# Transposing x on TensorE instead of through a DRAM copy and a DMA transpose, in an eight-core attention and quantised feed-forward kernel

## Chip, cores and metric

One Trainium2 chip, eight cores, one program. The 16 sequences are split two to a core; the cores exchange nothing. The metric is the device time in microseconds of the slowest core.

## The reference

For each sequence of 2048 tokens with 1024 features, in float32 (cut):

```python
q = x @ Wq.T + bq;  k = x @ Wk.T + bk;  v = x @ Wv.T + bv
scores = where(j > i, -inf, q @ k.T / 32)
attn = softmax(scores, axis=-2)
x = layernorm(x + attn @ v)
h = bit_linear(x, w1)                 # activations to 8 bits, weights to -1, 0, 1
h = silu(depthwise_conv1d(h) + conv_b)
x = layernorm(x + bit_linear(h, w2))
```

Every projection contracts over the 1024 features, so TensorE needs x with the features on the partitions, that is x transposed.

## The kernel before

The program is a list of operations with named resources; `Prog.build` turns the dependences into semaphore waits, engine by engine, in program order. Three of its rules matter here. A DMA waits for the DMA issued before it on the same engine's queue, so each queue has one transfer in flight. A DMA transpose (`xbar=True`) also waits for the last DMA of every other queue, and every later DMA waits for it. `fence(new, old)` makes the first use of each new name wait for all users of the old names, where two sets of tiles share memory.

Constants and zero padding come first (POOL issues 36 tiny stores, L352 to L362). Then the three attention weights are staged: eight tiles each of 128 rows are loaded by SP (L384), cast to bf16 by DVE (L387) and stored to DRAM by POOL (L390). Then `attn(b)` runs for the core's two sequences:

1. For 16 row tiles of x: SP loads 512 KB into `A_x32[it % 2]` (L397), DVE casts it into `A_xbf[it % 2]` (L400), POOL stores 256 KB to `s_xbf` in DRAM (L403). Then the bias row `bv` is loaded (L409) and spread over the partitions by PE and DVE (L413, L417).
2. SP transposes `s_xbf` into eight tiles `A_xT[e8]` of 128 features by 2048 tokens (L421, eight DMA transposes), then Wv into `A_WvT` (L431, eight more), and for the first sequence Wq and Wk too.
3. V (L442, 256 matmuls), Q and K (L461, 512 matmuls), each reading `A_xT`.
4. Scores and exponentials into `A_P`, which shares memory with `A_xT`, `A_WvT` and the bias tiles (L497 to L540).
5. The attention output, first layernorm and quantisation, by row tile (L560 on). Each tile ends with `pv_xpose_flush`: eight PE transposes (L551), by turns into the PSUM tiles `X6` and `X7`, eight ACT copies out of them (L555), and a POOL store.

After both sequences `prep()` quantises w1 and w2, `ffn_entry()` brings them in by DMA transposes, and 16 chunks of the feed-forward follow (L838 to L969).

Of the kernel before, what the change touches and what calls it, by code (L numbers as in the profile page):

```python
# [19 lines left out]
ECH = 8  # L20
# [144 lines left out]
def build_program(T=2048, NB=2, debug=False):  # L165
    nc = bass.Bass("TRN2", target_bir_lowering=False)
    NT = T // 128
    NCHUNK = T // 256
    p = Prog()
# [24 lines left out]
    s_xbf = dscr("s_xbf", [NB, T, E], BF16)  # L194
# [28 lines left out]
    iden_bf = P_("iden_bf", [128, 128], BF16)  # L223
# [29 lines left out]
    def mc(i):  # L253
# [3 lines left out]
    A_xT = [mem.at(OB + e * 4096, f"A_xT{e}", [128, T], BF16) for e in range(ECH)]  # L257
# [10 lines left out]
           for t in range(NT)]  # L268
# [6 lines left out]
    A_xbf = [mem.at(AT + 8192 + i * 2048, f"A_xbf{i}", [128, E], BF16)  # L275
             for i in range(2)]
# [47 lines left out]
    B = [pstack.enter_context(nc.psum_tensor(f"bank{i}", [128, 512], F32))  # L324
         for i in range(6)]
    X6 = pstack.enter_context(nc.psum_tensor("xb6", [128, 1024], BF16))
    X7 = pstack.enter_context(nc.psum_tensor("xb7", [128, 1024], BF16))
# [4 lines left out]
         writes=["idenf"])  # L332
# [3 lines left out]
         reads=["idenf"], writes=["maskneg"])  # L336
# [3 lines left out]
         reads=["idenf"], writes=["idenf"])  # L340
    p.op("DVE", lambda e: e.tensor_copy(out=iden_bf[:], in_=iden_f[:]),
         reads=["idenf"], writes=["idenb"])
# [7 lines left out]
    for b in range(NB):  # L350
        for e8 in range(ECH):
            p.op("POOL", lambda e, b=b, e8=e8: e.dma_start(  # L352
                out=s_xqT[b, e8, :, 0:8], in_=zpad[:]),
                reads=["zpad"], writes=[f"sxq_zh{b}_{e8}"], dma=True)
            p.op("POOL", lambda e, b=b, e8=e8: e.dma_start(
                out=s_xqT[b, e8, :, T + 8:T + 16], in_=zpad[:]),
                reads=["zpad"], writes=[f"sxq_zt{b}_{e8}"], dma=True)
    for b in range(NB):
        p.op("POOL", lambda e, b=b: e.dma_start(
            out=s_m1[b, 0:1].rearrange("(o a) -> o a", o=1), in_=misc[0:1, 60:61]),  # L360
            reads=["msczero"], writes=[f"sm1z{b}"], dma=True)
# [30 lines left out]
                reads=[f"xbf{i % 2}"], writes=[f"scr_{nm}_{i}"], dma=True)  # L392

    def attn(b):
        for it in range(NT):
            sl = slice(it * 128, (it + 1) * 128)
            p.op("SP", lambda e, sl=sl, it=it: e.dma_start(  # L397
                out=A_x32[it % 2][:], in_=x_d[b, sl, :]),
                writes=[f"x32_{it % 2}"], dma=True)
            p.op("DVE", lambda e, it=it: e.tensor_copy(  # L400
                out=A_xbf[it % 2][:], in_=A_x32[it % 2][:]),
                reads=[f"x32_{it % 2}"], writes=[f"xbf{it % 2}"])
            p.op("POOL", lambda e, sl=sl, it=it: e.dma_start(  # L403
                out=s_xbf[b, sl, :], in_=A_xbf[it % 2][:]),
                reads=[f"xbf{it % 2}"], writes=[f"sxbf{it}"], dma=True)
        p.fence([f"xT{e}" for e in range(ECH)]
                + [f"WvT{e}" for e in range(ECH)] + ["BVbc", "bvrow"],
                [f"P{jt}" for jt in range(NT)])
        p.op("SP", lambda e: e.dma_start(out=A_brow2[:],  # L409
                                         in_=bv_d.rearrange("(o a) -> o a", o=1)),  # L410
             writes=["bvrow"], dma=True)
        for h in range(2):
# [4 lines left out]
            p.op("DVE", lambda e, h=h: e.tensor_copy(  # L417
                out=A_BVbc[:, h * 512:(h + 1) * 512], in_=B[h][:]),
                reads=[f"B{h}"], writes=["BVbc"])
        for e8 in range(ECH):  # L420
            p.op("SP", lambda e, e8=e8: e.dma_start(  # L421
                out=A_xT[e8][:], in_=s_xbf[b, :, e8 * 128:(e8 + 1) * 128],
                transpose=True),
                reads=[f"sxbf{it}" for it in range(NT)],
                writes=[f"xT{e8}"], dma=True, xbar=True)
        wlist = [(s_wv, A_WvT, "WvT", "wv")]
        if b == 0:
            wlist += [(s_wq, A_WqT, "WqT", "wq"), (s_wk, A_WkT, "WkT", "wk")]
# [8 lines left out]
        for it in range(NT):  # L437
            g = it % 2
            bk0, bk1 = 2 * g, 2 * g + 1
            for h, bk in ((0, bk0), (1, bk1)):  # L440
                for e8 in range(ECH):
                    p.op("PE", lambda e, it=it, h=h, bk=bk, e8=e8: e.matmul(  # L442
                        out=B[bk][:],
                        lhsT=A_xT[e8][:, it * 128:(it + 1) * 128],
                        rhs=A_WvT[e8][:, h * 512:(h + 1) * 512],
                        start=(e8 == 0), stop=(e8 == ECH - 1)),
                        reads=[f"xT{e8}", f"WvT{e8}"], writes=[f"B{bk}"])
                p.op("DVE", lambda e, it=it, h=h, bk=bk: e.tensor_tensor(
                    out=A_v[it][:, h * 512:(h + 1) * 512], in0=B[bk][:],
                    in1=A_BVbc[:, h * 512:(h + 1) * 512], op=ALU.add),  # L450
                    reads=[f"B{bk}", "BVbc"], writes=[f"v{it}"])

        icw = min(512, T)
        for dstl, wTl, bc, nm in ((A_qT, A_WqT, bqc, "q"), (A_kT, A_WkT, bkc, "k")):
            wkey = "WqT" if nm == "q" else "WkT"
            for fc in range(ECH):
                for ic in range(T // icw):
                    bk = (fc * (T // icw) + ic) % 4
                    for e8 in range(ECH):
                        p.op("PE", lambda e, fc=fc, ic=ic, bk=bk, e8=e8,  # L460
                             wTl=wTl: e.matmul(  # L461
                            out=B[bk][:, 0:icw],
                            lhsT=wTl[e8][:, fc * 128:(fc + 1) * 128],
                            rhs=A_xT[e8][:, ic * icw:(ic + 1) * icw],
                            start=(e8 == 0), stop=(e8 == ECH - 1)),
                            reads=[f"xT{e8}", f"{wkey}{e8}"], writes=[f"B{bk}"])
                    p.op("ACT", lambda e, fc=fc, ic=ic, bk=bk, dstl=dstl,
                         bc=bc: e.activation(
                        out=dstl[fc][:, ic * icw:(ic + 1) * icw],
                        in_=B[bk][:, 0:icw],  # L470
                        func=AF.Identity, bias=bc[:, fc:fc + 1], scale=1.0),
                        reads=[f"B{bk}", "b" + nm + "c"],
                        writes=[f"{nm}T{fc}"])

        p.fence([f"P{jt}" for jt in range(NT)],
                [f"xT{e}" for e in range(ECH)] + [f"WvT{e}" for e in range(ECH)]
                + ["BVbc", "BVbc_use", "brow", "bvrow"])
        gchunk = 0
        for jt in range(NT):
# [175 lines left out]
    def prep():  # L655
# [2 lines left out]
                [f"P{jt}" for jt in range(NT)] + [f"v{t}" for t in range(NT)]  # L658
                + [f"qT{e}" for e in range(ECH)] + [f"kT{e}" for e in range(ECH)]
                + [f"WqT{e}" for e in range(ECH)] + [f"WkT{e}" for e in range(ECH)]  # L660
                + [f"WvT{e}" for e in range(ECH)] + [f"xT{e}" for e in range(ECH)]
                + ["xres", "xln0", "xln1", "xqstg", "xqbf", "pvx0", "pvx1",
                   "BVbc", "bvrow", "brow", "x32_0", "x32_1", "xbf0", "xbf1"])
        tiles = []
# [90 lines left out]
    def ffn_entry():  # L755
        newk = ([f"W1qT{e}" for e in range(ECH)]
                + [f"W2qT{c}" for c in range(HCH)]
                + [f"Fg{pr}_{s}" for pr in range(2) for s in range(HCH)]
                + [f"F_xq{pr}_{e}" for pr in range(2) for e in range(ECH)]
                + [f"fxlnt{pr}_{t}" for pr in range(2) for t in range(2)]  # L760
                + [f"fw{pr}" for pr in range(2)] + [f"fbc{pr}" for pr in range(2)]
                + ["sbc", "fs2seg", "Mx", "Mn", "flnt"]
                + [f"hs{i}" for i in range(2)] + [f"u{i}" for i in range(2)]
                + [f"fev{i}" for i in range(2)]
                + [f"D{k}_{pr}" for k in range(3) for pr in range(2)]
                + ["fcm0", "fcm1", "fcn0", "fcn1", "fm2", "fr2", "fs2v", "frs2"])
        oldk = ([f"P{jt}" for jt in range(NT)] + [f"v{t}" for t in range(NT)]
                + [f"qT{e}" for e in range(ECH)] + [f"kT{e}" for e in range(ECH)]
                + [f"xT{e}" for e in range(ECH)] + [f"WqT{e}" for e in range(ECH)]
                + [f"WkT{e}" for e in range(ECH)] + [f"WvT{e}" for e in range(ECH)]  # L770
                + ["xres", "xln0", "xln1", "xqstg", "xqbf", "pvx0", "pvx1",
                   "BVbc", "bvrow", "brow", "x32_0", "x32_1", "xbf0", "xbf1"]
                + [f"pin{i}" for i in range(4)] + [f"pap{u}" for u in range(32)]
                + ["pob0", "pob1", "m1ct", "mrow"]
                + [f"cmax{i}" for i in range(4)] + [f"csum{i}" for i in range(4)]
                + ["colsum", "msczero", "Mraw"])
        p.fence(newk, oldk)
        for e8 in range(ECH):
            p.op("SP", lambda e, e8=e8: e.dma_start(
                out=F_W1qT[e8][:], in_=s_w1i[:, e8 * 128:(e8 + 1) * 128],  # L780
                transpose=True),
                reads=[f"sw1ib{i}" for i in range(16)],
                writes=[f"W1qT{e8}"], dma=True, xbar=True)
        for c in range(HCH):
            p.op("SP", lambda e, c=c: e.dma_start(
                out=F_W2qT[c][:], in_=s_w2i[:, c * 128:(c + 1) * 128],
                transpose=True),
                reads=[f"sw2ib{i}" for i in range(16)],
                writes=[f"W2qT{c}"], dma=True, xbar=True)
# [358 lines left out]
```

How the kernel before makes its waits and increments, by code:

```python
            def section(_):  # L118
                waited = {f: 0 for f in self.ENGINES}
                for i, emit, inc, deps in ops:
                    want = {}
                    for d in deps:
                        f = openg[d]
                        v = cums[d]
                        if v > want.get(f, 0):
                            want[f] = v
                    for f, v in want.items():
                        if waited[f] < v:
                            eo.wait_ge(sems[f], v)
                            waited[f] = v
                    inst = emit(eo)
                    if inc:
                        inst.then_inc(sems[streams[i]], inc)
```

## Time and profile before

| | us |
|---|---|
| median of 2 runs | 3677.25 (3653.91 and 3700.6) |
| profiled execution, device time | 3621.03 |
| its span, slowest core (core 1) | 3619.5 |
| spans of the eight cores | 3602.0 to 3619.5 |

The span is the time from the first to the last instruction of a core; the other 1.5 us of the profiled execution lie around it. Engines are PE (TensorE), DVE (VectorE), ACT (ScalarE), POOL (GpSimd) and SP; a name with a q after it is the engine's instruction queue, where DMAs are issued. The chain of waits is followed back from the last instruction: at each step to what released it.

### The profile page before, as it was taken

To read this page: it belongs to the slowest core of one execution; us is meant where nothing else is said; L and a number is where in the kernel's file an instruction comes from. 1 tells how busy PE (TensorE), PEld (TensorE's weight loads), DVE (VectorE), ACT (ScalarE), POOL (GpSimd) and SP (SyncE) were. 2 spreads that over 40 slices of the span, in tenths; PEclk is the share of its full clock that TensorE was granted. 3 is DMA by queue.
4 is the path that set the end of the run, shared out by engine and by line. 5 is a ranking of instruction groups with operands and counts; after the bars stand their busy time and mean duration, and the time that the engine had idled before them with its cause. 6 is when DMAs were issued, how large, how long until landed. Compare 5 with 4: busy or idle time off the path is not lost.

```text
span 3619.5 us, 39595 instructions; the slowest of 8 cores (3602.0 to 3619.5 us)
## 1 busy us (share of the span) xinstructions
PE 2036.9 (56%) x10824; PEld 1128.8 (31%) x10824; DVE 1409.0 (39%) x3969; ACT 1208.1 (33%) x3042; POOL 185.1 (5%) x297
## 2 busy tenths in 40 slices
PE   0006984630996471000018777877777877778775
PEld 0002431210443120000005454544444544445442
DVE  0112025530204553333006544555544555554554
ACT  0000423320132332332006444444444444444442
POOL 2100000110000110011000000000000000000000
PEclk9999996765998575555558888877888878788887
DMA  0554002345000235876630000000000000000000
GB/s 25 197 169 76 1 1 73 105 129 130 6 1 12 93 108 197 294 260 201 124 76 23 30 30 24 19 19 30 30 30 25 18 18 30 30 30 27 16 18 18
DMA packets 201374, 248.20 MB, mean 69 GB/s; under 512 B 143106, under 2 KB 159682, under 8 KB 192964
## 3 DMA queue, kind: packets, MB, share of 16 engines
q1 hardware_dynamic: 174468, 138.61, 14.2%
q0 software_dynamic: 22080, 73.50, 5.9%
q10 hardware_dynamic: 4608, 33.56, 2.8%
q8 instruction: 92, 1.51, 0.2%
q14 instruction: 126, 1.03, 0.1%
HBM read 138.58 MB, written 73.48 MB: 59 GB/s over the span
## 4 chain that ended last, share of the span: by engine, by line
PE 36%; DMA 24%; DVE 17%; issue 10%; ACT 10%; POOL 1%; DVEq 1%; ACTq 0%; POOLq 0%; SPq 0%
PE bank L957 11%; PE bank L838 9%; PE bank L461 6%; DVE F_u L945 4%; DMA PR_in<-w 3%; PE bank L859 3%; PE bank L442 3%; DVE Fg L948 3%; DMA F_W2qT<-s_w2i 3%; DMA s_xbf<-A_xbf 3%; DMA s_w2i<-PR_ob 2%; DMA s_w1i<-PR_ob 2%; PE bank L497 2%; ACT F_D L851 2%; DMA A_xT<-s_xbf 2%
## 5 line engine op out<-in xcount | busy, mean ns | idle before, releaser
L838 PE MATMUL bank<-F_xq,F_W1qT 128*128 128x258 bf16 x4096 | 652.0, 312 | 0.0
L957 PE MATMUL bank<-F_W2qT,Fg 128*128 128x512 bf16 x2048 | 526.2, 395 | 45.6 <-ACT F_ev L969 39.2
L838 PEld LDWEIGHTS bank<-F_xq,F_W1qT 128*128 128x128 bf16 x4096 | 453.4, 111 | 180.6 <-issue 27.9
L864 ACT ACTIVATE Fg<-bank,cbc 128x256 bf16<-128x256 f32 x512 | 241.7, 472 | 741.0 <-PE bank L859 732.7
L859 PE MATMUL bank<-F_hs,F_D 128*128 128x256 bf16 x1536 | 286.8, 301 | 226.2 <-DVE F_hs L844 108.3
L844 DVE TENSOR_TENSOR F_hs<-bank,F_fbc 128x258 bf16<-128x258 f32 x512 | 217.1, 424 | 338.1 <-PE bank L859 306.6
L826 PE MATMUL bank<-F_fw,ones 1*128 1x258 f32 x32 | 18.6, 680 | 485.2 <-DVE F_fw L822 485.2
L957 PEld LDWEIGHTS bank<-F_W2qT,Fg 128*128 128x128 bf16 x2048 | 203.4, 100 | 261.6 <-issue 93.2
L859 PEld LDWEIGHTS bank<-F_hs,F_D 128*128 128x128 bf16 x1536 | 144.4, 104 | 312.6 <-issue 287.1
L876 DVE TENSOR_TENSOR F_Mx<-F_Mx,Fg 128x256 bf16<-128x256 bf16 x496 | 143.5, 289 | 204.7 <-ACT Fg L864 201.4
L945 DVE TENSOR_TENSOR F_u<-Fg,F_sbc 128x256 f32<-128x256 bf16 x512 | 214.1, 418 | 0.6
L851 ACT ACTIVATE F_D<-iden_f,w0c 128x128 bf16<-128x128 f32 x512 | 200.0, 391 | 17.2 <-DMA s_w2i<-PR_ob 17.2
L851 ACT ACTIVATE F_D<-iden_f,w1c 128x128 bf16<-128x128 f32 x512 | 199.3, 389 | 0.0
L851 ACT ACTIVATE F_D<-iden_f,w2c 128x128 bf16<-128x128 f32 x512 | 199.3, 389 | 0.0
L573 PE MATMUL bank<-A_v,A_P 128*128 128x512 bf16 x544 | 174.0, 489 | 28.4 <-DVE misc L531 14.5
L442 PE MATMUL bank<-A_WvT,A_xT 128*128 128x512 bf16 x512 | 121.2, 397 | 121.4 <-DMA A_WvT<-s_wv 121.4
L948 DVE TENSOR_SCALAR Fg<-F_u 128x256 bf16<-128x256 f32 x512 | 150.5, 294 | 56.8 <-DVE F_u L945 3.2
L413 PE MATMUL bank<-A_brow,ones 1*128 1x512 f32 x8 | 7.5, 1089 | 285.7 <-DMA A_brow<-bv 285.7
L497 PE MATMUL bank<-A_qT,A_kT 128*128 128x512 bf16 (+3 forms) x640 | 138.4, 373 | 45.1 <-ACT A_P L525 41.7
L826 PEld LDWEIGHTS bank<-F_fw,ones 1*128 1x128 f32 x32 | 7.7, 299 | 489.3 <-issue 489.3
L551 PE MATMUL xb<-iden_bf,PV_xqbf 128*128 128x128 bf16 x256 | 60.1, 249 | 172.8 <-DVE PV_xqbf L637 132.6
L879 DVE TENSOR_TENSOR F_Mn<-F_Mn,Fg 128x256 bf16<-128x256 bf16 x496 | 141.5, 285 | 0.7 <-DVE F_Mx L876 0.7
(131 smaller groups left out, 2003.4 us busy)
## 6 DMA issues: line engine op xcount, KB each, us to landing
PR_in<-w ACTq DMA_DIRECT2D x32, 1024.0 KB, 6.8
PR_in<-w SPq DMA_DIRECT2D x32, 1024.0 KB
A_x<-x SPq DMA_DIRECT2D x32, 512.0 KB
PV_xsrc<-x SPq DMA_DIRECT2D x32, 512.0 KB
s_xln<-PV_xln POOLq DMA_DIRECT2D x32, 512.0 KB, 3.3
F_xlnt<-s_xln SPq DMA_DIRECT2D x32, 512.0 KB
out<-F_xlnt POOLq DMA_DIRECT2D x32, 512.0 KB, 3.0
F_xq<-s_xqT SPq DMA_DIRECT2D x128, 64.5 KB
```

What stands on the lines that cost most here:

```text
L442: p.op("PE", lambda e, it=it, h=h, bk=bk, e8=e8: e.matmul(out=B[bk][:], lhsT=A_xT[e8][:, it * 128:(it + 1) * 128], rhs=A_WvT[e8][:, h * 51 ...
L461: wTl=wTl: e.matmul(out=B[bk][:, 0:icw], lhsT=wTl[e8][:, fc * 128:(fc + 1) * 128], rhs=A_xT[e8][:, ic * icw:(ic + 1) * icw], start=(e8 == ...
L497: p.op("PE", lambda e, e8=e8, jt=jt, cs=cs, w=w, bk=bk: e.matmul(out=B[bk][:, 0:w], lhsT=A_kT[e8][:, jt * 128:(jt + 1) * 128], rhs=A_qT[e8 ...
L573: p.op("PE", lambda e, it=it, jt=jt, h=h, bk=bk: e.matmul(out=B[bk][:], lhsT=A_P[jt][:, it * 128 - jt * 128: it * 128 - jt * 128 + 128], r ...
L838: p.op("PE", lambda e, s=s, e8=e8, bk=bk, par=par: e.matmul(out=B[bk][:, 0:258], lhsT=F_W1qT[e8][:, s * 128:(s + 1) * 128], rhs=F_xq[par][ ...
L844: p.op("DVE", lambda e, s=s, bk=bk, par=par: e.tensor_tensor(out=F_hs[s % 2][:], in0=B[bk][:, 0:258], in1=F_fbc[par][:], op=ALU.mult), rea ...
L851: p.op("ACT", lambda e, k=k, s=s, wc=wc: e.activation(out=F_D[k][s % 2][:], in_=iden_f[:], func=AF.Identity, scale=wc[:, s:s + 1]), reads= ...
L859: p.op("PE", lambda e, k=k, s=s: e.matmul(out=B[2][:, 0:256], lhsT=F_D[k][s % 2][:], rhs=F_hs[s % 2][:, k:k + 256], start=(k == 0), stop=( ...
L864: p.op("ACT", lambda e, s=s, par=par: e.activation(out=F_g[par][s][:], in_=B[2][:, 0:256], func=AF.Silu, bias=cbc[:, s:s + 1], scale=1.0), ...
L945: p.op("DVE", lambda e, cs=cs, par=par, up=up: e.tensor_tensor(out=F_u[up][:], in0=F_g[par][cs][:], in1=F_sbc[:], op=ALU.mult), reads=[f"F ...
L948: p.op("DVE", lambda e, cs=cs, par=par, up=up: e.tensor_scalar(out=F_g[par][cs][:], in0=F_u[up][:], scalar1=MAGIC, scalar2=MAGIC, op0=ALU. ...
L957: p.op("PE", lambda e, par=par, tb=tb, h=h, cs=cs, bk=bk: e.matmul(out=B[bk][:], lhsT=F_g[par][cs][:, tb * 128:(tb + 1) * 128], rhs=F_W2qT ...
```

## The change

Step 2 loses the transposes of x, and step 1 loses the stores. In the loop over the 16 row tiles, each cast tile is transposed by PE in eight blocks of 128x128, by turns into `X6` and `X7`, and ACT copies each block into its place in `A_xT[e8]`. The names `xT{e8}` become `xT{e8}_{t}`, one per row tile. Because `A_xT` is now written inside the loop, the fence against `A_P` moves ahead of the loop, and it now also covers `x32_0`, `x32_1`, `xbf0` and `xbf1`. The loads, the casts, the load of `bv`, the transposes of the weights and all matmuls of V, Q and K stay.

```diff
     def attn(b):
+        p.fence([f"xT{e}_{t}" for e in range(ECH) for t in range(NT)]
+                + [f"WvT{e}" for e in range(ECH)] + ["BVbc", "bvrow",
+                   "x32_0", "x32_1", "xbf0", "xbf1"],
+                [f"P{jt}" for jt in range(NT)])
         for it in range(NT):
...
-            p.op("POOL", lambda e, sl=sl, it=it: e.dma_start(
-                out=s_xbf[b, sl, :], in_=A_xbf[it % 2][:]),
-                reads=[f"xbf{it % 2}"], writes=[f"sxbf{it}"], dma=True)
-        p.fence([f"xT{e}" for e in range(ECH)]
-                + [f"WvT{e}" for e in range(ECH)] + ["BVbc", "bvrow"],
-                [f"P{jt}" for jt in range(NT)])
+            for e8 in range(ECH):
+                xb = X6 if e8 % 2 == 0 else X7
+                xk = "X6" if e8 % 2 == 0 else "X7"
+                p.op("PE", lambda e, it=it, e8=e8, xb=xb: e.transpose(
+                    out=xb[:, 0:128],
+                    in_=A_xbf[it % 2][:, e8 * 128:(e8 + 1) * 128],
+                    identity=iden_bf[:]),
+                    reads=[f"xbf{it % 2}", "idenb"], writes=[xk])
+                p.op("ACT", lambda e, it=it, e8=e8, xb=xb: e.copy(
+                    out=A_xT[e8][:, it * 128:(it + 1) * 128], in_=xb[:, 0:128]),
+                    reads=[xk], writes=[f"xT{e8}_{it}"])
...
-        for e8 in range(ECH):
-            p.op("SP", lambda e, e8=e8: e.dma_start(
-                out=A_xT[e8][:], in_=s_xbf[b, :, e8 * 128:(e8 + 1) * 128],
-                transpose=True),
-                reads=[f"sxbf{it}" for it in range(NT)],
-                writes=[f"xT{e8}"], dma=True, xbar=True)
...
-                        reads=[f"xT{e8}", f"WvT{e8}"], writes=[f"B{bk}"])
+                        reads=[f"xT{e8}_{it}", f"WvT{e8}"], writes=[f"B{bk}"])
```

The reads of the Q and K matmuls and the later fences take the new names.

## Rows read from the trace of the kernel before

**Rows 1.** The page: span; busy time; busy tenths in 40 slices; chain by engine and line.
```profile
span 3619.5 us, 39595 instructions; the slowest of 8 cores (3602.0 to 3619.5 us)
PE 2036.9 (56%) x10824; PEld 1128.8 (31%) x10824; DVE 1409.0 (39%) x3969; ACT 1208.1 (33%) x3042; POOL 185.1 (5%) x297
PE   0006984630996471000018777877777877778775
PE 36%; DMA 24%; DVE 17%; issue 10%; ACT 10%; POOL 1%; DVEq 1%; ACTq 0%; POOLq 0%; SPq 0%
PE bank L957 11%; PE bank L838 9%; PE bank L461 6%; DVE F_u L945 4%; DMA PR_in<-w 3%; PE bank L859 3%; PE bank L442 3%; DVE Fg L948 3%; DMA F_W2qT<-s_w2i 3%; DMA s_xbf<-A_xbf 3%; DMA s_w2i<-PR_ob 2%; DMA s_w1i<-PR_ob 2%; PE bank L497 2%; ACT F_D L851 2%; DMA A_xT<-s_xbf 2%
```

**Rows 2.** Chain of waits around the first sequence's x: start us, us, what.
```profile
227.92 0.50 issue
228.42 3.14 DMA s_xbf<-A_xbf
...
238.99 2.31 DMA s_xbf<-A_xbf
241.39 0.04 issue
241.43 4.38 DMA A_xT<-s_xbf
...
272.14 4.51 DMA A_xT<-s_xbf
276.71 3.37 DMA A_WvT<-s_wv
...
300.78 3.46 DMA A_WvT<-s_wv
304.23 0.14 issue
304.37 15.79 PE bank L442 x62
```

**Rows 3.** Timeline, first sequence: start us, us, engine, line, what, count [idle before <-releaser].
```profile
173.34 57.95 SPq L397 DMA_DIRECT2D A_x<-x  x16
234.86 0.24 SPq L409 DMA_DIRECT2D A_brow<-bv  x1
236.60 3.75 PE L413 MATMUL bank<-A_brow,ones 1*128 1x512 f32 x4 [223.09 <-DMA A_brow<-bv]
241.43 32.69 SPq L421 DMA_TRANSPOSE A_xT<-s_xbf  x8
276.71 25.21 SPq L431 DMA_TRANSPOSE A_WvT<-s_wv  x8
```

**Rows 4.** Timeline, second sequence: from the end of the attention before to WvT.
```profile
751.45 7.07 PE L573 MATMUL bank<-A_v,A_P 128*128 128x512 bf16 x32
778.94 1.27 DVE L400 CAST A_xbf<-A_x 128x1024 bf16<-128x1024 f32 x2
779.69 56.69 SPq L397 DMA_DIRECT2D A_x<-x  x14
787.42 0.53 POOL L648 DMA_DIRECT2D s_m<-mrow  x1 [6.73 <-DMA s_xqT<-PV_xqstg]
789.70 0.59 POOL L403 DMA_DIRECT2D s_xbf<-A_xbf  x1 [1.75 <-DMA s_m<-mrow]
792.23 0.69 DVE L400 CAST A_xbf<-A_x 128x1024 bf16<-128x1024 f32 x1 [12.02 <-DMA s_xbf<-A_xbf]
839.65 0.25 SPq L409 DMA_DIRECT2D A_brow<-bv  x1
841.26 3.75 PE L413 MATMUL bank<-A_brow,ones 1*128 1x512 f32 x4 [62.63 <-DMA A_brow<-bv]
847.22 32.69 SPq L421 DMA_TRANSPOSE A_xT<-s_xbf  x8
882.21 26.10 SPq L431 DMA_TRANSPOSE A_WvT<-s_wv  x8
```

**Rows 5.** SP's queue, single load issues: weights, then the second sequence's x.
```profile
13.21 0.36 SPq L384 DMA_DIRECT2D A_x<-wq  x1
17.84 0.35 SPq L384 DMA_DIRECT2D A_x<-wq  x1
21.71 0.33 SPq L384 DMA_DIRECT2D A_x<-wq  x1
25.57 0.33 SPq L384 DMA_DIRECT2D A_x<-wq  x1
...
784.02 0.33 SPq L397 DMA_DIRECT2D A_x<-x  x1
793.00 0.33 SPq L397 DMA_DIRECT2D A_x<-x  x1
```

**Rows 6.** Timeline and one line's instructions: the last transposes and copies after the attention.
```profile
775.34 0.39 PE L551 MATMUL xb<-iden_bf,PV_xqbf 128*128 128x128 bf16 x2 [9.13 <-DVE PV_xqbf L637]
775.69 3.13 ACT L555 COPY PV_xqstg<-xb 128x128 bf16<-128x128 bf16 x8 [4.44 <-PE xb L551]
L555 ACT COPY PV_xqstg<-xb x256: 265/266/268, 591.6 to 1383.4; 128x128 bf16<-128x128 bf16 x128
```

**Rows 7.** Stages by window: us, busy (x) of each engine, PEclk, DMA share, GB/s.
```profile
178.00:241.40 63.40, 3.75 (x4) 1.16 (x4) 12.37 (x18) 0.00 (x0) 9.17 (x17) 1.00 0.58 195
241.40:276.70 35.30, 0.00 (x0) 0.00 (x0) 0.00 (x0) 0.00 (x0) 0.00 (x0) 1.00 0.61 119
1935.00:2040.00 105.00, 81.08 (x489) 51.47 (x489) 56.96 (x189) 49.61 (x142) 1.70 (x3) 0.84 0.05 15
2355.00:2460.00 105.00, 79.95 (x459) 49.45 (x458) 54.82 (x183) 47.42 (x134) 2.26 (x4) 0.80 0.08 26
```

More of the change, by code:

```diff
@@ L465, in attn @@
                             start=(e8 == 0), stop=(e8 == ECH - 1)),
-                            reads=[f"xT{e8}", f"{wkey}{e8}"], writes=[f"B{bk}"])
+                            reads=[f"xT{e8}_{ic * icw // 128 + t}"
+                                   for t in range(icw // 128)]
+                            + [f"{wkey}{e8}"], writes=[f"B{bk}"])
                     p.op("ACT", lambda e, fc=fc, ic=ic, bk=bk, dstl=dstl,
@@ L475, in attn @@
         p.fence([f"P{jt}" for jt in range(NT)],
-                [f"xT{e}" for e in range(ECH)] + [f"WvT{e}" for e in range(ECH)]
+                [f"xT{e}_{t}" for e in range(ECH) for t in range(NT)]
+                + [f"WvT{e}" for e in range(ECH)]
                 + ["BVbc", "BVbc_use", "brow", "bvrow"])
@@ L660, in prep @@
                 + [f"WqT{e}" for e in range(ECH)] + [f"WkT{e}" for e in range(ECH)]
-                + [f"WvT{e}" for e in range(ECH)] + [f"xT{e}" for e in range(ECH)]
+                + [f"WvT{e}" for e in range(ECH)]
+                + [f"xT{e}_{t}" for e in range(ECH) for t in range(NT)]
                 + ["xres", "xln0", "xln1", "xqstg", "xqbf", "pvx0", "pvx1",
@@ L768, in ffn_entry @@
                 + [f"qT{e}" for e in range(ECH)] + [f"kT{e}" for e in range(ECH)]
-                + [f"xT{e}" for e in range(ECH)] + [f"WqT{e}" for e in range(ECH)]
+                + [f"xT{e}_{t}" for e in range(ECH) for t in range(NT)]
+                + [f"WqT{e}" for e in range(ECH)]
                 + [f"WkT{e}" for e in range(ECH)] + [f"WvT{e}" for e in range(ECH)]
```

## The prediction

> **What bounds the kernel now.** I read the page first. TensorE has the largest share of busy time, 56% of the span, but its row of 40 slices shows stretches where it does nothing at all, and the chain of waits puts 24% of the span on DMAs [rows 1]. So no one engine bounds the kernel; it goes from stage to stage, and each has its own limit. Among the chain's lines two belong to the operations that the change removes: the stores `s_xbf<-A_xbf` at 3% and the transposes `A_xT<-s_xbf` at 2% of 3619.5 us.
>
> Second I read the chain in order of time around the first sequence [rows 2]. From about 182 to 241 us it runs from store to store, then through eight transposes of x, then through eight of Wv, and only then into the V matmuls (L442). Nothing else is on it. Third, the windows: from 241.4 to 276.7 us not one of the five engines is busy for any time [rows 7]. The transposes of x hide nothing and nothing hides them.
>
> Fourth, the timelines of both sequences give the times at which the DMAs are issued [rows 3, 4]. These are what the sum is made from, because all that follows the first issue of `A_WvT` (its eight transposes, V, Q, K) is the same before and after.
>
> **First sequence.** The first transpose of Wv is issued at 276.71 us. After the change it waits for the load of `bv` on its own queue, and for the last POOL DMA, which is then a weight store long finished. `bv` is issued at 234.86 and released PE at 236.60 [rows 3]. If the loads of x keep their pace, the first Wv transpose is issued at 236.6: 276.7 - 236.6 = 40.1 us earlier. It has two parts: 276.71 - 241.43 = 35.3 for the eight transposes of x, and 241.43 - 236.60 = 4.8 for the last stores, which ran on behind `bv`.
>
> **Do the loads keep their pace?** The 16 loads and the wait of the last reach from 173.34 to 234.86, 61.5 us or 3.85 each [rows 3]. The chain runs through the stores, so the loads might be held back by them. But SP's queue shows weight loads of the same size at a time when POOL stores only 2 KB pieces: issued at 17.84, 21.71 and 25.57, so 3.87 and 3.86 apart [rows 5]. I take 3.85: load and store happened to be equally slow, and taking the store away leaves the load. What it costs the other way is a rival below.
>
> **What is added per tile.** Eight PE transposes and eight ACT copies, 128 of each per sequence. The same work stands after the attention, with the same alternation of `X6` and `X7`: eight copies from first start to last end in 3.13 us, each 0.266 us long, so one every (3.13 - 0.27)/7 = 0.41 us, and the first transpose starts 0.35 us ahead of the first copy [rows 6]. A tile alone takes 0.35 + 3.13 = 3.5 us; in a steady stream 8 x 0.41 = 3.3 us. Both are below 3.85, PE and ACT have nothing else to do then (PE busy 3.75 us and ACT 0 of 63.4 [rows 7]), and two `A_xbf` buffers let tile it+1 be cast while tile it is transposed. I cost them at nothing. The cover is the load; without it they would cost the 3.3 us a tile. The last tile's 3.5 us and PE's 3.75 us for the bias rows (L413) come after the last load, some 8 us with the cast, but they lie beside the eight Wv transposes, which take 304.2 - 276.7 = 27.5 us [rows 2]. The first V matmul needs the first of these, but its group ends with the eighth. An activation table load at ACT's first instruction falls in the wait for the first tile.
>
> **Second sequence.** Here a further stall goes. DVE's third cast waits 12.02 us for a store of x, which stood on POOL's queue behind the store of `s_m`, which had waited 6.73 us for the store of `s_xqT` [rows 4]. SP therefore issues its load at 793.00 and not some 3.9 us after the one at 784.02 [rows 5]. With no store of x the cast needs only the load and the PE transposes two tiles before. The 14 loads from 779.69 then take 4.33 (to 784.02, as seen) and 13 x 3.85 = 50.1 us: `bv` is issued at 834.1 instead of 839.65. It lands 841.26 - 839.65 = 1.6 us later, at 835.7, and the Wv transpose that was issued at 882.21 is issued then: 46.5 us earlier. Its parts are 882.21 - 847.22 = 35.0 for the transposes of x, 847.22 - 841.26 = 6.0 for the last stores, 5.6 for the stall.
>
> **The moved fence.** The first two loads of the second sequence now wait for the last attention matmul, which ends at 751.45 + 7.07 = 758.5 us. Behind them on SP's queue stand only the other loads of x. Two loads at 4.63 at most (the slowest issue to issue, 13.21 to 17.84 [rows 5]) land by 767.8, and DVE cannot cast before 778.94, when its own queue is through with the layernorm [rows 4]. Cost nothing, with 11 us to spare; were that cover gone, each load would cost its 3.85. For the first sequence the fence is empty. The finer names `xT{e8}_{t}` add at most waits that are already satisfied: PE has waited for nearly all the copies when it transposes the last tile.
>
> **The sum.** 40.1 + 46.5 = 86.6 us. Against the profiled execution: 3621.0 - 86.6 = 3534 us. The median of the runs shown is 56 us above that execution, and the two runs differ by 47 us, so against the median it is 3677.25 - 86.6 = 3590.6 us, 2.4% less. I give 3591. A difference of 2%, about what a measurement of this kernel can tell from no change, is 73.5 us.
>
> **A page against the trace.** The eight transposes of x take 4.4 us each for 512 KB [rows 2], at 119 GB/s [rows 7]. The Trainium skill (DMA: Bandwidth & Descriptors, section Latency and other measured facts) gives DMA transposes an effective 261 GB/s, which would be an estimated 2.0 us each. By the page the sum would be 86.6 - 70.3 + 32 = 48 us, within 2%; the trace has the duration itself, and it decides.
>
> **The rivals.**
>
> *The loads speed up.* The stores did: the last one, with no load beside it, took 2.31 us where the one at 228.42 took 3.14 [rows 2]. If the loads fell below 3.3 us, the copies would set the pace at 3.28, and 14 + 13 tiles would each save 0.57 us: 15.4 us more, 102 in all, 3575 us. Against it speak the weight loads at 3.86 [rows 5]. Chance 0.14. Beside it stands a rule of the Trainium skill (DMA: Bandwidth & Descriptors, section Anatomy of one DMA, measured on the GpSimd path): 2.0 us plus the bytes over 436 GB/s, here an estimated 3.2 us for a load. The 3.86 of the rows disagrees with it.
>
> *The hand-over per tile costs more.* PE and ACT wake each other 16 times a tile. If the pace came to 4.3 us, 0.45 x 29 tiles = 13 us would go, and the change would fall within 2%; at 5 us the gain is 86.6 - 33 = 53 us, 3624. For it speaks how little lies between 3.5 and 3.85; against it, that eight copies in the same pattern kept 0.41 us. Chance 0.11.
>
> *The feed-forward's clock.* It is half of the span, and its granted clock, a mixture of the levels 1.2 and 2.4 GHz, lies between 0.80 and 0.84 in stretches of 105 us, with PE 80 us busy [rows 7]. A mean lower by 0.02 costs up to 80 x 0.02/0.82 = 2.0 us in each of 16, 31 us in all, and leaves 55: 3622 us. Nothing in the change reaches that stage, but the runs shown differ by as much. Chance 0.08.
>
> *The stages of a tile stop overlapping,* the way to a slower kernel. If load, cast, transposes and copies ran one after the other, a tile would cost 3.85 + 0.69 + 3.5 = 8.0 us, 4.2 more, 122 us over 29 tiles: 35 us slower than before, 3713. It decides from 86.6/29 = 3.0 us more a tile, that is 6.85, and is slower by 2% only from 9.4. Against it stand the two buffers for x and for the cast. Chance 0.02.
>
> *The transposes were hidden anyway.* The empty window [rows 7] excludes it but for 0.01.
>
> **How the numbers follow.** The likeliest, 0.64, is the sum, with a gain of 77 to 93 us. Faster by over 2% takes nearly all of it (0.62) and the faster loads (0.14): 0.76. Within 2%: 0.02 of the first, 0.11, 0.08, 0.01 and most of the serial case: 0.23. Slower: 0.01. The range runs from the sum against the profiled execution, 3534, rounded down to 3530 for loads that gain a little, up to 3640, which holds the slow hand-over and the clock. It leaves out the serial case, the hidden one, and the faster loads where they fall together with runs as fast as the profiled one.
>
> **What would show it.** In the changed profile `s_xbf<-A_xbf` and `A_xT<-s_xbf` are gone, 128 transposes and copies per sequence lie between the loads, and these still come 3.85 us apart: right on the pace. The first Wv transpose at about 237 us and, 86.6 us earlier than before, at about 796 in the second sequence: right on the sum. No 12 us wait of a cast: right on the stall. Casts that wait for PE, or PE for ACT, with loads over 4.3 us apart, would show the hand-over wrong. The Q and K matmuls and the feed-forward should last as long as before; if they don't, the sum is wrong in a place it doesn't look at.

## The result and the profile after

The changed kernel takes 0.968 of the time of the kernel before (95% interval 0.965 to 0.972): medians of all runs 3520.7 and 3627.3 us, about 115 us by the ratio. In some executions one die ran at a lower granted clock and took longer; the medians count them, the ratios here do not. The profiled executions took 3512.2 and 3621.0 us; their spans, as means over the eight cores, are 3499.4 and 3608.2, 108.8 us apart. Faster was forecast, but by 87 us and not under 3530: the gain is larger by a quarter to a third, and the time lies below the range.

The page of the changed kernel, its span, busy times and the chain by line; the two entries that [rows 1] shows for `s_xbf` are gone:

```profile
span 3510.7 us, 40780 instructions; the slowest of 8 cores (3488.6 to 3510.7 us)
PE 2097.0 (60%) x11080; PEld 1155.2 (33%) x11080; DVE 1408.5 (40%) x3969; ACT 1267.2 (36%) x3298; POOL 167.0 (5%) x265
PE bank L965 11%; PE bank L846 9%; PE bank L464 6%; DVE F_u L953 4%; PE bank L867 3%; DMA PR_in<-w 3%; PE bank L445 3%; DVE Fg L956 3%; DMA A_x<-x 3%; DMA F_W2qT<-s_w2i 3%; DMA s_w1i<-PR_ob 3%; PE bank L503 3%; DMA s_w2i<-PR_ob 2%; ACT F_D L859 2%; DMA s_xqT<-zpad 2%
```

Its chain of waits around the first sequence's x (start us, us, what), the counterpart of [rows 2]:

```profile
203.59 3.34 DMA A_x<-x
...
214.03 3.13 DMA A_x<-x
...
217.28 3.35 DMA A_x<-x
...
220.70 1.56 DMA A_brow<-bv
222.30 0.04 issue
222.34 3.17 DMA A_WvT<-s_wv
```

The chain now goes from load to load, and from `bv` straight to Wv. SP's queue of the same core, both sequences, beside [rows 3, 4]:

```profile
165.75 51.85 SPq L401 DMA_DIRECT2D A_x<-x  x16
220.70 0.24 SPq L418 DMA_DIRECT2D A_brow<-bv  x1
222.34 25.34 SPq L434 DMA_TRANSPOSE A_WvT<-s_wv  x8
...
705.09 69.55 SPq L401 DMA_DIRECT2D A_x<-x  x16
778.08 0.25 SPq L418 DMA_DIRECT2D A_brow<-bv  x1
779.65 20.95 SPq L434 DMA_TRANSPOSE A_WvT<-s_wv  x7
```

From these marks, as means over the eight cores, comes the table on which the rest of this text leans. The last column is the prediction's term.

| stretch | before | after | gained | forecast |
|---|---|---|---|---|
| start to the first load of x (the weights) | 171.9 | 164.1 | 7.8 | 0 |
| 16 loads of x, to the issue of `bv` | 62.4 | 54.9 | 7.5 | 0 |
| `bv` to the first Wv transpose | 42.2 | 1.5 | 40.7 | 40.1 |
| to `bv` of the second sequence | 563.2 | 555.3 | 7.9 | 5.6 |
| `bv` to Wv, second sequence | 43.2 | 1.6 | 41.6 | 40.9 |
| to the quantisation of w1 | 505.7 | 503.8 | 1.9 | 0 |
| to the feed-forward and its end | 2219.6 | 2218.2 | 1.4 | 0 |

The transposes and the waits for the last stores went as worked out. Of the 22 us that the sum does not have, 15 lie in the DMAs ahead of them, and 8 of these where the two programs do the same.

How close the added work comes to being the limit stands in the waits of the changed kernel, 170 to 222 us (who waited for whom, us in total, times, longest):

```profile
DVE A_xbf L404 <- DMA A_x<-x: 22.0, 8, 3.4
...
PE xb L410 <- ACT A_xT L415: 17.8, 50, 1.7
DVE A_xbf L404 <- PE xb L410: 15.7, 6, 2.9
```

Eight casts waited last for their load, six for the transposes two tiles back; the chain above still goes from load to load without a break. PE transposes in pairs, 0.77 us from pair to pair, 3.1 us a tile, against a load every 3.43. The work is hidden, but only by 0.3 us a tile.

### The profile page after: what moved, and what is told of

It reads as the page before. It is cut to its first block, busy times and chain, and to the rows that moved or that the text cites. A ratio compares the mean times of both kernels' runs of the same rounds, so it can differ in the third digit from the quotient of the medians.

```text
span 3510.7 us, 40780 instructions; the slowest of 8 cores (3488.6 to 3510.7 us)
## 1 busy us (share of the span) xinstructions
PE 2097.0 (60%) x11080; PEld 1155.2 (33%) x11080; DVE 1408.5 (40%) x3969; ACT 1267.2 (36%) x3298; POOL 167.0 (5%) x265
## 4 chain that ended last, share of the span: by engine, by line
PE 38%; DMA 23%; DVE 18%; ACT 10%; issue 9%; POOL 1%; DVEq 1%; ACTq 0%; POOLq 0%; SPq 0%
PE bank L965 11%; PE bank L846 9%; PE bank L464 6%; DVE F_u L953 4%; PE bank L867 3%; DMA PR_in<-w 3%; PE bank L445 3%; DVE Fg L956 3%; DMA A_x<-x 3%; DMA F_W2qT<-s_w2i 3%; DMA s_w1i<-PR_ob 3%; PE bank L503 3%; DMA s_w2i<-PR_ob 2%; ACT F_D L859 2%; DMA s_xqT<-zpad 2%
## 5 line engine op out<-in xcount | busy, mean ns | idle before, releaser
L410 PE MATMUL xb<-iden_bf,A_xbf 128*128 128x128 bf16 x256 | 57.8, 265 | 211.7 <-DVE A_xbf L404 174.3
L503 PE MATMUL bank<-A_qT,A_kT 128*128 128x512 bf16 (+3 forms) x640 | 138.2, 373 | 46.0 <-ACT A_P L531 42.2
```

The source lines that it names most:

```text
L503: p.op("PE", lambda e, e8=e8, jt=jt, cs=cs, w=w, bk=bk: e.matmul(out=B[bk][:, 0:w], lhsT=A_kT[e8][:, jt * 128:(jt + 1) * 128], rhs=A_qT[e8 ...
```

## The experiments

Ratios are to the kernel before, measured beside each. Stretches are means over the cores of one profile each; "weights by" is the time at which the first load of x is issued. Four theories were at issue:

- A: the stores of x slow the loads beside them.
- B, later called S: the DMAs of the kernel before were slow by the chance of one sitting on one chip.
- P: their speed is a property of the program, for one because DMA transposes of `s_xbf` are in it; D narrows that to those that write `A_xT`.
- L: the make-up of the program sets the speed of its early DMAs.

**before_again, before_third, after_again, after_third** are the two kernels unchanged.

> The kernel before, unchanged, profiled again. In its first profile the 16 loads of x of the first sequence came 3.85 us apart and the first was issued at 173.3 us; in the changed kernel they come 3.43 apart and the first at 163.0 on the same core, although nothing ahead of it was changed. Theory A (the stores of x slow the loads, and only they): the loads of the weights and of x are as slow here as in the first profile, first load of x at 170 to 175 us, loads 3.85 apart, undisturbed weight loads at 17 to 26 us 3.86 apart. Theory B (all DMAs of the first profile were slower, whatever the kernel): first load of x at 163 to 166, undisturbed weight loads 3.3 to 3.6 apart, span 10 to 20 us below 3619.

> The kernel before a third time, on this chip. Theory P: weights staged by 172 us, first 16 loads of x in 62 us, as in both profiles so far. Theory S: anywhere between 164 and 175.

> The changed kernel, unchanged, measured beside the others. In its first profile the weights were staged by 164.1 us (mean over the cores of the issue of the first load of x), in both profiles of the kernel before by 171.9 and 171.8, though nothing differs up to there; in the two variants that differ only later, by 166.8 and 165.9. Theory P (a property of the program): 164 to 165 again, loads of x 3.4 us apart, ratio 0.968. Theory S (of the sitting): 166 to 172, loads 3.5 to 3.7 apart, ratio 0.968 to 0.975.

> The changed kernel a third time, on the same chip. Theory P: weights staged by 164 to 165 us, first 16 loads of x in 55 us. Theory S: as slow or as fast as the kernel before on this chip.

Weights by 171.8 and 173.8 us, 16 loads in 62.6 and 65.6 for the kernel before; 165.0 and 165.8, 55.4 and 55.5 for the changed one. after_again measured 0.968 (0.963 to 0.973), as at first. The undisturbed weight loads, second to fourth, come 3.78, 3.88 and 3.82 us apart in the three profiles of the kernel before and 3.50, 3.59 and 3.65 in those of the changed one. On four sittings neither kernel showed the other's speed. It belongs to the program, then, and theories B and S are out.

**stores_back, stores_back_2.** In the changed kernel:

```diff
+            p.op("POOL", lambda e, sl=sl, it=it: e.dma_start(
+                out=s_xbf[b, sl, :], in_=A_xbf[it % 2][:]),
+                reads=[f"xbf{it % 2}"], writes=[f"sxbf{it}"], dma=True)
             for e8 in range(ECH):
```

> The changed kernel with the 32 stores of the cast x to DRAM put back; nothing reads them. They bring back the wait of the first Wv transpose for the last store (4.8 and 6.0 us in the trace of the kernel before) and the stall behind the store of s_m (5.6 us), 16 us in all. Theory A (stores slow the loads): in addition the loads of x go from 3.43 to about 3.85 apart, 0.42 x 30 = 13 us more, so 29 us slower than the changed kernel, ratio to the kernel before about 0.976. Theory B (they don't): loads stay near 3.45 apart, 16 us slower than the changed kernel, ratio about 0.973.

> stores_back again, beside dead_transposes on the same chip. It had 166.8 us for the weights, 58.3 us for the first 16 loads of x, ratio 0.974. Both theories expect the same again within 2 us; if it now shows 172 and 62, the speed of the DMAs is one of the sitting.

0.974 (0.972 to 0.977) and 0.977 (0.972 to 0.981). On the chip where both were profiled, the mean span of the cores is 3527.4 us against 3504.9 for the changed kernel, 22.5 us more: between what theory B had (16) and theory A (29). The wait between `bv` and Wv is 7.0 and 8.0 us in the two sequences instead of 1.5, as both theories had it. The 16 loads take 58.3 and 58.5 us, 3.65 each: neither 3.45 nor 3.85. Why they take that, the chain of stores_back shows (start us, us, what):

```profile
178.41 2.81 DMA s_xbf<-A_xbf
181.33 0.49 issue
181.82 2.82 DMA s_xbf<-A_xbf
184.74 0.48 issue
185.22 2.79 DMA s_xbf<-A_xbf
```

It runs from store to store, as before the change [rows 2], but with 2.8 to 3.5 us a store where that had 3.0 to 3.6. Stores cost 0.2 us a tile, 3.1 us over the 16 loads. The other 0.25 of a tile came from somewhere else.

**only_first.** The second sequence goes the old way:

```diff
+            if b == 1:
+                p.op("POOL", lambda e, sl=sl, it=it: e.dma_start(
+                    out=s_xbf[b, sl, :], in_=A_xbf[it % 2][:]),
...
+                continue
             for e8 in range(ECH):
...
+        if b == 1:
+            for e8 in range(ECH):
+                p.op("SP", lambda e, e8=e8: e.dma_start(
+                    out=A_xT[e8][:], in_=s_xbf[b, :, e8 * 128:(e8 + 1) * 128],
+                    transpose=True),
```

> The change made for the first sequence only; the second stores, transposes by DMA and waits as before (but with the moved fence). By the traces the first sequence gives 40.7 us between the load of bv and the first Wv transpose, and 7.4 us in the pace of the loads of x: 48 us, ratio 0.987. If the faster weight staging comes with the change (Theory P), 8 us more: ratio 0.985. The second sequence keeps its 12 us wait of the third cast, its loads 3.8 apart and 43 us between bv and Wv.

0.991 (0.988 to 0.995), 32 us and not 48. In the first sequence there are 1.5 us between `bv` and Wv: the 40.7 are gained. But the weights took until 178.8 us and the 16 loads 65.3, with no store beside them. Its slowest core (SP's queue) shows it beside the changed kernel's above:

```profile
180.41 63.09 SPq L401 DMA_DIRECT2D A_x<-x  x16
247.05 0.24 SPq L423 DMA_DIRECT2D A_brow<-bv  x1
248.50 25.42 SPq L447 DMA_TRANSPOSE A_WvT<-s_wv  x8
```

The instructions of the first sequence are those of the changed kernel, and a load takes 4.1 us, where after_again on the same chip has 3.5. Theory A falls as the whole answer: without the stores the loads are no faster here. That they are the limit here, and were not before the change, the waits of the casts show (us in total, times, longest; first the kernel before, core 1, from 182 to 236 us, then only_first, core 3, from 182 to 246):

```profile
DVE A_xbf L400 <- DMA s_xbf<-A_xbf: 43.8, 14, 3.5
DVE A_xbf L404 <- DMA A_x<-x: 43.1, 13, 3.6
```

**before_placed.** In the kernel before, `s_xbf` is declared last:

```diff
-    s_xbf = dscr("s_xbf", [NB, T, E], BF16)
     s_xqT = dscr("s_xqT", [NB, ECH, 128, T + 16], BF16)
...
+    s_xbf = dscr("s_xbf", [NB, T, E], BF16)
```

> The kernel before with s_xbf declared last among the DRAM scratch tensors, so that the tensors behind it lie 8 MB lower; no instruction differs. If where the scratch lies sets the speed of the DMAs, the weight staging ends at 164 to 167 us instead of 172 and the loads of x come under 3.7 apart: 8 to 12 us faster, ratio 0.997. If not, everything is as in the kernel before, ratio 1.000.

There is no ratio; the profile has a mean span of 3612.0 us, the weights by 173.3 us and the loads in 63.7. The place of this scratch tensor does not make them quick.

**dead_transposes.** stores_back with eight transposes of `s_xbf` beside the second sequence's scores, into a free region:

```diff
+        if b == 1:
...
+                p.op("SP", lambda e, e8=e8: e.dma_start(
+                    out=A_dead[e8][:],
+                    in_=s_xbf[b, :, e8 * 128:(e8 + 1) * 128],
+                    transpose=True),
```

> stores_back with eight DMA transposes of s_xbf added beside the scores of the second sequence, into memory that nothing reads; they hide behind about 110 us of scores. So far every program with DMA transposes of s_xbf (the kernel before twice, before_placed, only_first) staged the weights by 172 to 179 us and had its first 16 loads of x 3.9 to 4.1 apart, even only_first, whose first sequence stores nothing, and every program without them by 164 to 167 us and 3.4 to 3.7 apart. Theory P (their presence in the program slows DMAs that run long before them): 172 or more, 3.9 apart, 10 us slower than stores_back, ratio 0.977. Theory S (chance of the sittings): 165 to 169 us, 3.5 to 3.7 apart, ratio 0.974.

0.978 (0.968 to 0.987), too wide to tell the theories apart, but 165.7 and 58.1 us, as stores_back. Theory P falls in the form that the mere presence of such transposes slows the early DMAs.

**both_ways.** stores_back with the transposes of x at their old place too:

```diff
+        for e8 in range(ECH):
+            p.op("SP", lambda e, e8=e8: e.dma_start(
+                out=A_xT[e8][:], in_=s_xbf[b, :, e8 * 128:(e8 + 1) * 128],
+                transpose=True),
+                reads=[f"sxbf{it}" for it in range(NT)],
+                writes=[f"xT{e8}_{t}" for t in range(NT)],
+                dma=True, xbar=True)
         wlist = [(s_wv, A_WvT, "WvT", "wv")]
```

> stores_back with the DMA transposes of x at their old place too: x is transposed on PE and then once more by DMA into the same A_xT. PE and ACT do the work of the changed kernel, the DMAs are those of the kernel before. By the trace the transposes come back whole, 35 us a sequence: about 70 us slower than stores_back. Theory D (the DMAs that read s_xbf into A_xT slow the DMAs ahead of them): weights staged by 172 us, loads of x 3.9 apart, ratio 1.000 or more. Theory L (it goes with the layout of the program: every fast one has the 256 transposes and 256 copies in it, the half-way one has 128): 164 to 167 us, 3.6 apart, 82 us of transposes and waits but not the rest come back, ratio 0.994 to 0.996.

0.999 (0.997 to 1.001). The transposes come back whole: 43.6 and 44.4 us between `bv` and Wv. So nearly all of the gain that was worked out is theirs and their waits'. But the weights are done by 166.5 us and the loads take 59.1, the fast values, with every old DMA in place. That speaks against theory D. The ratio, which goes by the slowest core, does not show these 9 us (theory L had it at 0.994 to 0.996). The mean span of the eight cores does: 3617.1 us in the 9 executions that the ratio uses, against 3625.1 in the 17 of the kernel before beside it, 8.0 us less, give or take 5.

**before_padded, before_late_pad.** The kernel before with idle work: 256 transposes of the identity and 256 copies at the start, or 592 transposes at the quantisation of w1, 1390 us in.

```diff
+    for k in range(256):
+        xb, xk = (X6, "X6") if k % 2 == 0 else (X7, "X7")
+        p.op("PE", lambda e, xb=xb: e.transpose(
+            out=xb[:, 0:128], in_=iden_bf[:], identity=iden_bf[:]),
+            reads=["idenb"], writes=[xk])
+        p.op("ACT", lambda e, xb=xb: e.copy(
+            out=A_WkT[0][:, 0:128], in_=xb[:, 0:128]),
+            reads=[xk], writes=["WkT0"])
```

> The kernel before with 256 PE transposes of the identity and 256 ACT copies into memory that is overwritten later, run at the start, where PE and ACT wait for 170 us; 0.4 us each, 105 us in all, hidden. No DMA differs. Theory L: weights staged by 164 to 167 us, 16 loads of x in 58, some 12 us faster than the kernel before, ratio 0.996 to 0.997. Theory D, or neither: 172 to 174 us and 62 to 66, ratio 1.000.

> The kernel before with 592 PE transposes of the identity beside the quantisation of the weights, about 1390 us in, where PE is idle for 450 us; as matmul and weight load they bring the program from 39595 to about 40780 instructions, the count of the changed kernel. Nothing differs before 1390 us. Theory L (the make-up of the program, not what runs, sets the speed of the early DMAs): weights staged by 164 to 168 us, the first 16 loads of x in 57 to 59, 8 to 12 us faster, ratio 0.997. If it takes work that runs early: 172 to 174 us, 62 to 66, ratio 1.000.

before_padded: 0.999 (0.996 to 1.002), weights by 170.0 us, loads in 57.2. The loads are as theory L had them, the weights halfway. before_late_pad: 0.994 (0.991 to 0.998), 168.0 and 59.4, near what theory L had. Its slowest core beside [rows 3] (SP's queue):

```profile
165.88 54.07 SPq L397 DMA_DIRECT2D A_x<-x  x16
223.30 0.24 SPq L409 DMA_DIRECT2D A_brow<-bv  x1
229.82 35.05 SPq L421 DMA_TRANSPOSE A_xT<-s_xbf  x8
```

With matmuls in the program that do nothing and run 1200 us later, the loads of x take 3 us less than in any profile of the kernel before, and the staging 4. The profiles together, without all_pe, sorted by the instructions that the page of each counts:

| program | instructions | weights by | 16 loads |
|---|---|---|---|
| before, three profiles; before_placed | 39595 | 171.8 to 173.8 | 62.4 to 65.6 |
| only_first | 40185 | 178.8 | 65.3 |
| two_queues, fills_late (below) | 40722, 40780 | 165.9, 99.2 (zero stores moved) | 58.5, 56.5 |
| after, three profiles (no stores) | 40780 | 164.1 to 165.8 | 54.9 to 55.5 |
| before_late_pad | 40781 | 168.0 | 59.4 |
| stores_back twice, dead_transposes, both_ways | 40905 to 40949 | 165.7 to 166.8 | 58.1 to 59.1 |
| before_padded | 41129 | 170.0 | 57.2 |

The larger programs have the faster loads, the smaller ones the slow ones, with nothing measured between 40185 and 40722 instructions. On one chip after_again, only_first and before_placed had their 16 loads in 55.4, 65.3 and 63.7 us, on another before_third, after_third and stores_back_2 in 65.6, 55.5 and 58.5; so it goes with the program. That it is the make-up and not a DMA of the change, theory L, rests on both_ways, before_padded and before_late_pad. These ran on two chips on which the kernel before left no profile, so a quick chip is not excluded by a trace. Against it speak the mean spans beside the kernel before: 8.0 us less for both_ways, 3.9 (give or take 4.6) for before_padded and 14.5 (6.7) for before_late_pad, half of which its faster start does not explain. Nor is every early DMA quick: the undisturbed weight loads come 3.82 us apart in both_ways and 3.89 in before_late_pad, as in the kernel before. Theory L fits best and is not shown. How a program's make-up would reach its DMAs (where its code or the runtime's buffers come to lie in memory is one guess) was not tried and stays open.

**two_queues.** In the changed kernel, loads by turns on SP and ACT, two in flight, and copies out of X7 on DVE:

```diff
+            p.op("SP" if it % 2 == 0 else "ACT",
...
+                if e8 % 2 == 0:
+                    p.op("ACT", lambda e, it=it, e8=e8, xb=xb: e.copy(
...
+                else:
+                    p.op("DVE", lambda e, it=it, e8=e8, xb=xb: e.tensor_copy(
```

> The changed kernel with the loads of x by turns on SP's and ACT's queue, two in flight, and the copies out of X7 on DVE instead of ACT. If a load is mostly fixed time (one in flight keeps the DMA engines busy only part of the time), the loads of a sequence come 1.8 to 2.4 us apart instead of 3.43 and the PE and copy chain, halved in copies per engine, sets about 2.3: 28 tiles x 1.1 = 30 to 35 us faster than the changed kernel, ratio 0.959 to 0.960. If the loads are bound by bandwidth, they stay at 3.3 or more and the time is that of the changed kernel, 0.968.

0.973 (0.970 to 0.976): not the forecast gain. The interval overlaps that of the changed kernel, so slower is not shown by the total, but the 16 loads take 58.5 us where that had 54.9 to 55.5. The timeline of core 4 (start us, us, engine, line, what [idle before <-releaser]) says why:

```profile
182.77 0.69 DVE L409 CAST A_xbf<-A_x 128x1024 bf16<-128x1024 f32 x1
183.71 0.37 PE L417 MATMUL xb<-iden_bf,A_xbf 128*128 128x128 bf16 x2 [1.22 <-DVE A_xbf L409]
...
186.51 0.23 DVE L428 COPY A_xT<-xb 128x128 bf16<-128x128 bf16 x1 [0.54 <-PE xb L417]
186.68 0.69 DVE L409 CAST A_xbf<-A_x 128x1024 bf16<-128x1024 f32 x1
```

The next cast now stands behind this tile's copies on DVE's queue. Cast, transposes and copies run one after the other, 3.91 us from cast to cast. No cast waits for a load any more, so the question about the loads was not answered here. This is half of the prediction's rival in which the stages of a tile stop overlapping, brought about by moving four copies a tile to the engine of the casts.

**fills_late.** In the changed kernel, the 36 zero stores are issued ahead of the first sequence's scores:

```diff
-    for b in range(NB):
-        for e8 in range(ECH):
...
+        if b == 0:
+            zero_fills()
         gchunk = 0
```

> The changed kernel with POOL's 36 tiny zero stores moved from the start to the scores of the first sequence. At the start they hold the first weight store until 88 us, when the third cast could be ready at 26 us. If they only hold the weight staging, all of it shifts: 88 - 18 = about 65 to 70 us faster than the changed kernel, ratio 0.949 to 0.951. If they cost as much where they go (POOL has 110 us of scores for their 80 us, and the first attention store waits behind them), the gain is smaller.

0.951 (0.949 to 0.953), as forecast, some 63 us below the changed kernel by the two ratios. The first load of x is issued at 99.2 us instead of 164 to 166. In the changed kernel the zero stores, most 1.7 us long, follow one another on POOL's queue and hold the first weight store until 88.4 us (core 7). The prediction, which began at x, had not looked at this stall.

**all_pe.** fills_late without any DRAM copy or DMA transpose in the attention: weights, too, are loaded, cast and transposed on PE; eight transposes fill one PSUM tile, which one copy of 1024 columns empties, by turns on ACT and DVE; the next cast stands ahead of that copy; two loads in flight.

```diff
+        def stage(k):
+            xpose_tile(pars[k])
+            if k + 1 < len(tl):
+                cast_tile(pars[k + 1])
+                if k + 3 < len(tl):
+                    pars[k + 3] = load_tile(tl[k + 3][0])
+            _, dst, width, i, keys = tl[k]
+            evac_tile(pars[k], dst, i, keys)
```

> The changed kernel carried further: the zero fills late, and the weights loaded once, cast and transposed on PE like x, with no copy in DRAM and no DMA transpose in the attention; Wv and x first, the tiles of Wq and Wk between the V groups; loads by turns on SP and ACT; eight transposes into one PSUM bank and one copy of 1024 columns, by turns on ACT and DVE, with the next cast ahead of it. V of the first sequence can start after 24 tiles: at 2.3 us a tile 13 + 55 = 68 us, at 3.4 us 95 us, instead of 158 in fills_late. In the second sequence 24 tiles take 55 to 82 us instead of 35 + 28 of x and Wv now, so it gains or loses 10 to 20. Wq and Wk add some 20 us to the V stretch. Sum against fills_late: 50 to 90 us faster, ratio to the kernel before 0.926 to 0.938. If two loads in flight do not come faster than one, the loads set 3.4 a tile and it is 40 us faster than fills_late, 0.94.

0.920 (0.915 to 0.924), 3345 us: the fastest of all and faster than the 0.926 to 0.938 forecast, 0.95 of the changed kernel by the two ratios, some 63 us of which are fills_late's. PE's timeline:

```profile
69.01 1.01 PE L403 MATMUL xb<-iden_bf,A_xbf 128*128 128x128 bf16 x8 [1.73 <-DVE A_xbf L395]
71.80 1.01 PE L403 MATMUL xb<-iden_bf,A_xbf 128*128 128x128 bf16 x8 [1.78 <-DVE A_xbf L395]
...
86.67 5.48 PE L475 MATMUL bank<-A_WvT_all,A_xT_all 128*128 128x512 bf16 x16
```

V starts at 86.7 us; in the changed kernel its first group waits for the eighth Wv transpose until 250. A tile takes about 2.7 us, with 1.01 us of PE instead of 3.1: two loads in flight do come faster than one, and a copy for every eight transposes takes the alternation away. Several things changed at once here, and what each is worth alone was not measured.

## Why the prediction was right, and where it was wrong

**Right: what the chain showed.** The reading that nothing hides the transposes of x held to 1 us: 40.7 and 41.6 us where 40.1 and 40.9 were worked out, and both_ways gives them back. The stall went too: no cast of the second sequence waits for a store, and the stretch up to its `bv` is 7.9 us shorter where 5.6 was forecast. That the two are near is in part luck: the stalled load, 9.8 us from issue to issue, still takes 5.6 after the change and gives 4.2 us, and the quicker pace of the other loads, which the sum did not have, gives 3.5 (means over the cores). The moved fence cost nothing: the two first loads of the second sequence land before DVE's cast (first issue 705.09, cast at 722.99 on core 7). The rival that the transposes were hidden is out.

**Wrong: "I take 3.85".** The measured 3521 us lie below the range of 3530 to 3640. The step that failed is the pace of the loads. It came from three weight loads of the kernel before, 3.86 us apart with no stores of size beside them [rows 5], and was treated as the price of a load. It was the price of a load in that program, and the 3.85 of the loads of x themselves was the pace of the stores, for which every cast waited. Measured in the changed kernel: 3.43, 3.46 and 3.47. Of the 7.5 us on the first 16 loads, the stores take 3.1 (58.4 against 55.3 us in programs of nearly the same size); the rest, some 4, comes with the program, by a cause that stays open. The rival that loads speed up had the right direction and a chance of 0.14. Its floor of 3.28 was set too high, since the transposes and copies of a tile took 3.1 us, but no load came down to it. The range left this rival out where it falls together with runs as fast as the profiled one, 3621.0 - 102 = 3519 us, and there the time fell, though the 102 did not come from that mechanism alone.

The Trainium skill's rule that stood beside that rival (DMA: Bandwidth & Descriptors, section Anatomy of one DMA: 2.0 us plus bytes over 436 GB/s, given for the GpSimd path, an estimated 3.2 us here) is nearer than my row was: the changed kernel's chain shows loads of 3.13 to 3.47 us and one of 3.93, on SP's queue. In only_first, with loads of 3.8 to 4.7 us (core 1), it is not. The Trainium skill's rate for DMA transposes (same page, section Latency and other measured facts) disagrees with the runs: the eight transposes cost 35 us a sequence in the kernel before, 36.5 in both_ways against stores_back, and not the 16 estimated from the rate.

**Wrong: "all that follows is the same" was applied to what comes ahead as well.** The sum let the first 172 us stand, since no instruction there changes. They shrank by 7.8. By before_padded and before_late_pad, where they shrank by 2 and 4 with every old DMA in place, at least a part need not come from anything in the change itself. No row of the kernel before could have told it; the range could have held it, but its lower end was set by the sum alone and gave the DMAs outside the change no play.

**The reference time.** 56 us lay between the profiled execution and the median shown. The latter fell to 3627 with more runs. The forecast of 3591 took it as it stood; against the profiled execution the same sum gave 3534. Like against like, profiled execution against profiled execution, the gain is 108.8 us and the sum 86.6: 15.3 of the difference are the two points above, 3.6 lie in the terms of the sum, 3.3 after them.

**The hand-over** was judged rightly, at nothing, but the margin is 0.3 us a tile, and two_queues shows how easily the overlap behind it is lost.

## What to carry to other kernels

A stretch in which no engine is busy and the chain names one queue is worth its full length: read the two issue times at its ends, and here the sum held to a microsecond. The price of a DMA read in one program is no constant for another: give it 10% either way in the range, for the DMAs that the change does not touch too. Read also which engine's wait sets a pace before taking it for the price of an operation. Before transposing on PE, put the next cast ahead of the copies on its queue (two_queues lost by the opposite), and fill a whole PSUM tile before emptying it (in all_pe, among other changes).

## What the runs showed of the hardware that I had not expected

The same load of 512 KB, with the same instructions ahead of it, took 3.5 us in one program and 4.1 in another on the same chip (after_again, only_first). With 592 idle matmuls placed 1200 us later it took 3.7 where the kernel before had 3.9 to 4.1, and the program ran 0.6% faster (0.2 to 0.9%), though these loads were compared across chips, and the quicker start explains less than half of that. Nothing in the instructions that ran until then tells the programs apart.
